# Slot logits for three images as one product of 32 columns, with the masking operation reading them three times

## The chip, the cores and the metric

The kernel runs on one core of one Trainium2 chip, in float32 throughout. The metric is the device time of one execution in microseconds (us). Engines go by short names: PE is the matrix engine (its weight loads are listed as PEld), DVE the vector engine, ACT the scalar engine, POOL the GpSimd engine, SP the engine that issues the DMAs.

## The reference, cut to what matters

A small vision model in three stages: patches are normalised and projected to tokens (32 images, 36 tokens each, 192 channels); attention over channels with a residual and a layer norm; then a soft mixture of experts with 8 experts of 4 slots. The change lies in the last stage:

```python
Xn = l2_normalize(X, axis=-1)                       # X: [32, 36, 192]
sp = l2_normalize(slot_params, axis=1) * scale      # [192, 8, 4]
logits = jnp.einsum('bmd,dnp->bmnp', Xn, sp)        # 32 logits for each token
D = softmax(logits, axis=1)                         # over the tokens of one image
C = softmax(logits.reshape(b, m, 32), axis=2)       # over the 32 slots of one token
X_tilde = einsum('bmd,bmnp->bnpd', Xn, D); ...      # experts on the slots
Y = jnp.einsum('bnpd,bmnp->bmd', Y_tilde, C)
```

The slots `sp` are the same for all images.

## The kernel before, in words

The images are worked in 11 groups of three (`NG = 11`, `GI = 3`; the last group has two). A group is 108 tokens, which lie on 108 partitions. So that one set of operations serves three images, a group's router works on a matrix of 108 tokens by 96 columns, 96 being 3 images times 32 slots, in which only the block of a token's own image counts; everything else gets -1e30 added (`negmask`) before the exponentials.

The slots are prepared once: `slot_sums`, `slot_root` and `slot_scale` normalise them, and a loop of three vector operations (L779 to L782) writes them three times side by side into `sp3`, a tile of 96 partitions and 2 x 3 x 32 elements (the 192 channels are split into two halves of 96, index `f`).

For each group g the router then runs:

- `turn_xn` (L579, PE) turns the unit tokens, and `take_xn` (L1111, ACT) copies them to `xnT`.
- `logits` (L593, PE): for each half f, `xnT` is the weight operand (96 rows by 108 columns) and `sp3[:, f]` the moving operand of 96 columns. A float32 product is two PE instructions in the profile, so a group has 4 of them, and 11 groups 44. They write `ps[0:108, 6, 0:96]`.
- `mask_logits` (L890, DVE) adds `negmask` to the 96 columns and writes `lm`.
- `turn_l` (L606, PE), the maxima `max_c` and `max_d` (L897, L905, DVE), the exponentials (L1118, L1126, ACT), `invert_sums` and `scale_d` (L912, L913, L918, DVE), `turn_dc` (L622, L623, PE), `take_d` (L926, DVE) and `slot_in` (L634, PE).

The experts follow: `hidden` (L649, PE), `gelu`, `spread` (L935, DVE), then `slot_out` (L664, PE), `slot_bias`, `combine` (L677, PE) and a last layer norm.

No planner runs: each engine has a fixed list of calls, written out by hand (PE at L680 to L699, DVE at L983 to L1036), and works it in that order; semaphores tell it when an input is there. The products of the attention stage of later groups are interleaved with the router of earlier ones. The slots are prepared at the `slot_scale()` of L991, long before `logits(0)` at L686.

Of the kernel before, what the change touches and what calls it, by code (L numbers as in the profile page):

```python
# [25 lines left out]
ALU = mybir.AluOpType  # L26
# [10 lines left out]
GI = 3  # L37
NG = (B + GI - 1) // GI
NT = NTOK // 128
F = D // 2  # L40
R = D - 128
NE, NP = 8, 4
SL = NE * NP
# [9 lines left out]
def images(g):  # L53
    return min(GI, B - g * GI)


def tokens(g):
    return images(g) * TOK
# [16 lines left out]
def build(nc, x, x_t, w_tok, ln1_gb, ln2_g, ln2_b, g2col, b2col, w_qk, w_v, w_rest, w_proj, b_proj, temp, slots, scale,  # L75
# [3 lines left out]
    with ctx:  # L79
        def sb(name, shape):  # L80
            return ctx.enter_context(nc.sbuf_tensor(name, shape, F32))

        def sem(name):
            return ctx.enter_context(nc.semaphore(name))
# [4 lines left out]
        negmask = sb("negmask", [128, GI * SL])  # L89
# [16 lines left out]
        spsq = sb("spsq", [F, 2, NE, NP])  # L106
        spn = sb("spn", [F, 2, NP])
        spe = sb("spe", [F, 2, NP])
        sp3 = sb("sp3", [F, 2, GI, NE, NP])
        scl = sb("scl", [F, 1])  # L110
        wd = sb("wd", [F, 2, NE, 32])
        bd = sb("bd", [128, 2])
# [49 lines left out]
        NX = 3  # L162
        xnT = sb("xnT", [F, NX, 2, GI * TOK])
        lm = sb("lm", [128, NX, GI * SL])
# [24 lines left out]
        ps = ctx.enter_context(nc.psum_tensor("ps", [128, 8, 512], F32))  # L189
# [38 lines left out]
            return ps[0:F, 5, 0:2 * GI * TOK].rearrange("p (f n) -> p f n", f=2)[:, :, 0:tokens(g)]  # L228

        def lgp(g):  # L230
            return ps[0:tokens(g), 6, 0:images(g) * SL]

        def ltp(g):
            return ps[0:images(g) * SL, 6 if g < GS else 0, 0:tokens(g)]
# [44 lines left out]
        sp_ready = sem("sp_ready")  # L279
# [52 lines left out]
        lm_ready = sem("lm_ready")  # L332
# [115 lines left out]
        def _(pe):  # L448
# [134 lines left out]
            def logits(g):  # L583
                pe.wait_ge(xnT_ready, g + 1)
                if g == 0:
                    pe.wait_ge(sp_ready, 1)
                    pe.wait_ge(y1_ready, NT)
                if 1 <= g <= GS:
                    pe.wait_ge(eD_ready, g)
                if g > GS:  # L590
                    pe.wait_ge(lm_ready, g)
                for f in range(2):
                    mm = pe.matmul(lgp(g), xnT[:, g % NX, f, 0:tokens(g)],  # L593
                                   sp3[:, f, 0:images(g), :, :].rearrange("p i n q -> p (i n q)"),
                                   start=f == 0, stop=f == 1)
                mm.then_inc(lgp_ready, 1)

# [86 lines left out]
            project(1); qkv(5); mix(2); norms(4); turn_h(7); project(2); qkv(6); mix(3); gram(4)  # L684
            norms(5); turn_h(8); project(3); qkv(7); mix(4); norms(6); gram(5); turn_xn(0); project(4)
            logits(0); qkv(8); mix(5); norms(7); gram(6); turn_l(0); turn_xn(1); project(5); qkv(9)  # L686
            mix(6); gram(7); norms(8); logits(1); turn_dc(0); turn_xn(2); project(6); turn_l(1)
            norms(9); gram(8); qkv(10); gram(9); logits(2); turn_xn(3); mix(7); turn_l(2); slot_in(0)
            turn_xn(4); norms(10); logits(3); project(7); turn_dc(1); turn_l(3); logits(4); turn_xn(5)
            mix(8); slot_in(1); turn_xn(6); turn_l(4); logits(5); turn_dc(2); project(8); turn_l(5)  # L690
# [12 lines left out]
        def _(dve):  # L703
# [64 lines left out]
            def slot_scale():  # L768
                dve.wait_ge(sp_root, 1)
                dve.tensor_scalar(spn[:, :, :], spe[:, :, :], EPS_L2, None, ALU.add).then_inc(sp_eps, 1)  # L770
                dve.wait_ge(sp_eps, 1)
                dve.reciprocal(spe[:, :, :], spn[:, :, :]).then_inc(sp_inv, 1)
                dve.wait_ge(sp_inv, 1)
                for f in range(2):
                    ins = dve.tensor_tensor(spsq[:, f, :, :], spraw[:, f, :, :],
                                            spe[:, f, :].unsqueeze(1).broadcast_to([F, NE, NP]), ALU.mult)
                ins.then_inc(sp_scaled, 1)
                dve.wait_ge(sp_scaled, 1)
                for i in range(GI):  # L779
                    ins = dve.tensor_scalar(sp3[:, :, i, :, :].rearrange("p f n q -> p f (n q)"),  # L780
                                            spsq[:, :, :, :].rearrange("p f n q -> p f (n q)"),
                                            scl[:, 0:1], None, ALU.mult)  # L782
                ins.then_inc(sp_ready, 1)

            def scales(g):
                ni = images(g)
# [93 lines left out]
                                  ALU.mult, ALU.mult).then_inc(xn_ready, 1)  # L880

            def mask_logits(g):
                n, s = tokens(g), images(g) * SL
                dve.wait_ge(lgp_ready, g + 1)
                if g >= NX:
                    dve.wait_ge(eC_ready, g - NX + 1)
                    dve.wait_ge(ltp_ready, g - NX + 1)
                if g == 0:
                    dve.wait_ge(negmask_in, 16)
                dve.tensor_tensor(lm[0:n, g % NX, 0:s], lgp(g), negmask[0:n, 0:s], ALU.add).then_inc(lm_ready, 1)  # L890

            def max_c(g):
                n, s = tokens(g), images(g) * SL
# [95 lines left out]
            token_moments(4); x_stats(6); slot_sums(); x_moments(6); token_out(5); turn_p(0); x_stats(7)  # L989
            token_stats(5); token_out(6); x_moments(7); token_moments(5); x_stats(8); x_moments(8)  # L990
            scales(1); y_sums(0); token_stats(6); scores(1); slot_scale(); score_max(1); ln2_norm(4)  # L991
            y_norm(0); token_moments(6); score_shift(1); token_out(7); ln2_norm(5); turn_p(1)
            token_stats(7); scales(2); ln2_norm(6); scores(2); token_moments(7); residual(0)
# [5 lines left out]
            scores(4); score_max(4); residual(3); score_shift(4); h1(1); h1_length(1); turn_p(4)  # L999
            h1_length(2); scales(5); unit_h1(0); h1_inverse(1); h1(2); y_sums(4); unit_h1(1); y_norm(4)  # L1000
            scores(5); score_max(5); residual(4); mask_logits(0); score_shift(5); residual_stats(3)
            turn_p(5); residual_stats(4); residual_moments(3); scales(6); h1_inverse(2); y_sums(5)
            y_norm(5); unit_h1(2); scores(6); h1(3); residual_moments(4); score_max(6); max_d(0)
            score_shift(6); max_c(0); residual(5); h1_length(3); turn_p(6); residual_stats(5)
            h1_length(4); scales(7); h1(4); invert_sums(0); scale_d(0); h1_inverse(3); y_sums(6)
            residual_moments(5); scores(7); y_norm(6); mask_logits(1); max_c(1); score_max(7)
            unit_h1(3); score_shift(7); scales(8); residual(6); max_d(1); h1_length(5); h1(5)
            residual_stats(6); turn_p(7); scores(8); h1_inverse(4); residual_moments(6); unit_h1(4)
            h1_inverse(5); invert_sums(1); score_max(8); scale_d(1); score_shift(8); take_d(0)
            h1_length(6); unit_h1(5); scales(9); mask_logits(2); h1(6); scores(9); h1_inverse(6)  # L1010
            y_sums(7); max_d(2); unit_h1(6); score_max(9); max_c(2); y_norm(7); score_shift(9)
            turn_p(8); mask_logits(3); invert_sums(2); max_c(3); scale_d(2); residual(7); take_d(1)
# [339 lines left out]
```

## Time and profile before

| | |
|---|---|
| time, median of 3 runs | 112.63 us (112.24 to 112.75) |
| the profiled execution's own time | 112.18 us |
| its span, first to last instruction | 110.4 us |
| PE busy | 101.7 us, 92% |
| DVE busy | 87.7 us, 79% |
| ACT busy | 67.5 us, 61% |
| POOL busy | 53.4 us, 48% |

The span is the stretch that the trace covers; 1.8 us of the profiled execution's time lie around it. A busy PE is one that has an instruction in its pipeline: the instructions overlap, so the mean duration of one is longer than the distance at which one follows another. To read that distance (the pitch), divide a stretch of equal instructions on the chain of waits by their number, or compare two starts in the timeline.

### The profile page before, as it was taken

How to read it: one execution, taken by the hardware profiler on the slowest of the kernel's cores; microseconds unless marked ns; L12 is line 12 of the kernel's file. 1: busy time of each engine (PE TensorE's matmuls, PEld its weight loads, DVE VectorE, ACT ScalarE, POOL GpSimd, SP SyncE). 2: the span in 40 equal slices, each digit the busy share in tenths (PEclk: the TensorE clock that was granted, in tenths of full speed). 3: DMA queues.
4: the chain of work that ended last, by engine and by line, in shares of the span. 5: the costliest groups of instructions: out<-in, count | busy, mean ns of one | idle time of the engine just before them, and what ended most of it. 6: DMA issues, size and time to landing. Idle time of an engine off the chain costs nothing. (4 is left out here: it accounts for less than half of the span.)

```text
span 110.4 us, 4479 instructions
## 1 busy us (share of the span) xinstructions
PE 101.7 (92%) x1607; PEld 88.2 (80%) x1607; DVE 87.7 (79%) x380; ACT 67.5 (61%) x222; POOL 53.4 (48%) x126
## 2 busy tenths in 40 slices
PE   6999999999999999999999999799989989999900
PEld 6999989979999887887898887679779668879500
DVE  2129756968998958958977989999999897999960
ACT  4000023729563887798887996787785994476570
POOL 8800552263999887847204417906030340076880
PEclk9999999999999999999999999999999999999996
DMA  2999999469501111111000000010042000002232
GB/s 23 334 339 394 389 386 398 153 212 342 235 0 30 36 32 40 29 35 32 6 3 6 0 6 0 6 48 24 30 105 72 7 0 3 0 6 84 66 112 58
DMA packets 8554, 11.27 MB, mean 102 GB/s; under 512 B 2358, under 2 KB 5878, under 8 KB 8534
## 3 DMA queue, kind: packets, MB, share of 16 engines
q1 hardware_dynamic: 8533, 11.00, 29.5%
q8 instruction: 13, 0.21, 0.8%
q14 instruction: 8, 0.06, 0.2%
HBM read 9.22 MB, written 0.88 MB: 92 GB/s over the span
## 5 line engine op out<-in xcount | busy, mean ns | idle before, releaser
L480 PE MATMUL ps<-wc,xT 128*128 128x192 f32 x108 | 19.1, 330 | 0.0
L480 PEld LDWEIGHTS ps<-wc,xT 128*128 128x128 f32 x108 | 17.4, 190 | 0.7 <-issue 0.6
L1046 ACT ACTIVATE hT<-ps,b,g 128x128 f32<-128x128 f32 x18 | 7.3, 463 | 16.4 <-PE ps L491 16.3
L1068 ACT ACTIVATE km<-ps,imgsel 108x192 f32<-108x192 f32 (+1 forms) x32 | 11.1, 420 | 3.7 <-PE ps L515 3.6
L1256 POOL TENSOR_SCALAR mv<-mv 108x1 f32<-108x1 f32 (+1 forms) x11 | 3.0, 270 | 14.4 <-DVE mv L856 14.4
L568 PE MATMUL ps<-wp,yT 128*108 128x192 f32 (+1 forms) x44 | 9.3, 333 | 0.0
L664 PE MATMUL ps<-wu,hb 128*96 128x192 f32 (+1 forms) x44 | 9.2, 332 | 0.1
L1261 POOL TENSOR_TENSOR r<-mv,halves 108x2 f32<-108x2 f32 (+1 forms) x11 | 8.8, 803 | 0.8
L508 PE MATMUL ps<-wqk,hT 128*108 128x192 f32 (+1 forms) x44 | 9.0, 326 | 0.0
L726 DVE BATCH_NORM_STATS2 st<-xs 128x6 f32<-128x384 f32 x18 | 8.9, 537 | 0.0
L1249 POOL TENSOR_TENSOR rqt<-rn,tempc 128x6 f32<-128x6 f32 x11 | 2.2, 199 | 12.1 <-ACT rn L1105 12.1
L1207 POOL TENSOR_SCALAR var<-mv 128x1 f32<-128x1 f32 x9 | 2.0, 219 | 11.8 <-DVE mv L731 11.5
L1078 ACT ACTIVATE sqk<-km 108x576 f32<-108x576 f32 (+1 forms) x11 | 7.5, 683 | 0.0
L664 PEld LDWEIGHTS ps<-wu,hb 128*96 128x96 f32 (+1 forms) x44 | 6.5, 161 | 0.8 <-issue 0.4
L593 PE MATMUL ps<-sp,xnT 96*108 96x96 f32 (+1 forms) x44 | 6.2, 264 | 0.7 <-ACT xnT L1111 0.4
L568 PEld LDWEIGHTS ps<-wp,yT 128*108 128x108 f32 (+1 forms) x44 | 6.4, 170 | 0.5 <-DVE yT L836 0.2
L559 PE MATMUL ps<-vT,pc 32*32 32x37 f32 x512 | 6.8, 195 | 0.0
L1162 ACT ACTIVATE o<-z,sh,rstd 108x192 f32<-108x192 f32 x10 | 5.1, 543 | 2.8 <-DVE sh L980 2.8
L1269 POOL TENSOR_TENSOR rstd<-var,mhalf 108x1 f32<-108x1 f32 (+1 forms) x11 | 6.3, 576 | 0.9
L506 PE MATMUL ps<-hT,wv 128*128 128x108 f32 (+1 forms) x44 | 6.6, 273 | 0.0
L559 PEld LDWEIGHTS ps<-vT,pc 32*32 32x32 f32 x512 | 5.5, 104 | 1.3
L508 PEld LDWEIGHTS ps<-wqk,hT 128*108 128x108 f32 (+1 forms) x44 | 6.4, 171 | 0.0
(118 smaller groups left out, 296.6 us busy)
## 6 DMA issues: line engine op xcount, KB each, us to landing
xT<-in_x_t SPq DMA_DIRECT2D x9, 384.0 KB, 6.4
xs<-in_x SPq DMA_DIRECT2D x9, 384.0 KB, 6.2
out<-o SPq DMA_DIRECT2D x10, 81.0 KB
wt<-in_w_tok SPq DMA_DIRECT2D x2, 288.0 KB, 3.2
wqk<-in_w_qk SPq DMA_DIRECT2D x1, 192.0 KB, 5.9
wp<-in_w_proj SPq DMA_DIRECT2D x1, 192.0 KB, 10.0
wd<-in_w_down SPq DMA_DIRECT2D x1, 192.0 KB
z<-h SPq DMA_DIRECT2D x2, 81.0 KB
```

Source lines behind the costliest of these rows:

```text
L480: mm = pe.matmul(tokp(t), xT[:, o + kc * 128:o + (kc + 1) * 128], wc[:, kc, :], start=kc == 0, stop=kc == KC - 1)
L506: pe.matmul(vp(g)[:, m, :], wv[:, m, :], main, start=True, stop=False)
L508: pe.matmul(qkp(g)[:, m, :], main, wqk[:, m * D:(m + 1) * D], start=False, stop=False)
L559: mm = pe.matmul(yp(g)[r, m, i, :], pc[r, g % 2, GI * m + i, :], vT[r, m, g * GI + i, :], start=True, stop=True, tile_position=(32 * j, 32 ...
L568: mm = pe.matmul(prp(g), yT[:, g % NY, m, 0:images(g), :].rearrange("p i n -> p (i n)"), wp[:, m, :], start=m == 0, stop=m == 1)
L664: mm = pe.matmul(ytp(g), hb[:, e, i0:i0 + ni, :, :].rearrange("p i n q -> p (i n q)"), wu[:, e, :], start=e == 0, stop=e == 1)
L726: ins = dve.bn_stats(st1[:, t % 2, h, :], xs[:, t % NB, h * (PD // 2):(h + 1) * (PD // 2)])
L1046: ins = act.activation(hT[:, f, t * 128:(t + 1) * 128], htp(t)[:, f, :], ACT.Identity, bias=b2[:, f:f + 1], scale=g2[:, f:f + 1])
L1068: act.activation(km[0:n, g % NK, i, :], qkp(g)[:, 1, :], ACT.Copy, scale=imgsel[0:n, i:i + 1])
L1078: act.activation(sqk[0:n, g % 2, 0:ni, :], km[0:n, g % NK, 0:ni, :], ACT.Square).then_inc(sqk_ready, 1)
L1261: pool.tensor_tensor(r3[0:n, g, :], mv3[0:n, g, 1:3], halves[0:n, :], ALU.pow).then_inc(r3_ready, 1)
L1269: pool.tensor_tensor(rstd4[0:n, g:g + 1], var4[0:n, g:g + 1], mhalf[0:n, 0:1], ALU.pow).then_inc(rstd4_ready, 1)
```

## The change

The slots are stored once (`spk`, 2 x 32 elements a partition). The moving operand of `logits` has 32 columns instead of 96 (64 in the last group), and the product fills 32 columns of PSUM. The masking operation reads these 32 columns once for each image of the group, by a middle dimension of stride 0, and writes 96 columns as before. Two of the three vector operations that stored the slots are gone. Semaphores, the order of the calls and everything behind `lm` stay as they are.

```diff
-        sp3 = sb("sp3", [F, 2, GI, NE, NP])
+        spk = sb("spk", [F, 2, NE, NP])
...
         def lgp(g):
-            return ps[0:tokens(g), 6, 0:images(g) * SL]
+            return ps[0:tokens(g), 6, 0:SL]
...
                     mm = pe.matmul(lgp(g), xnT[:, g % NX, f, 0:tokens(g)],
-                                   sp3[:, f, 0:images(g), :, :].rearrange("p i n q -> p (i n q)"),
+                                   spk[:, f, :, :].rearrange("p n q -> p (n q)"),
                                    start=f == 0, stop=f == 1)
...
-                for i in range(GI):
-                    ins = dve.tensor_scalar(sp3[:, :, i, :, :].rearrange("p f n q -> p f (n q)"),
-                                            spsq[:, :, :, :].rearrange("p f n q -> p f (n q)"),
-                                            scl[:, 0:1], None, ALU.mult)
-                ins.then_inc(sp_ready, 1)
+                dve.tensor_scalar(spk[:, :, :, :].rearrange("p f n q -> p f (n q)"),
+                                  spsq[:, :, :, :].rearrange("p f n q -> p f (n q)"),
+                                  scl[:, 0:1], None, ALU.mult).then_inc(sp_ready, 1)
...
-                dve.tensor_tensor(lm[0:n, g % NX, 0:s], lgp(g), negmask[0:n, 0:s], ALU.add).then_inc(lm_ready, 1)
+                dve.tensor_tensor(lm[0:n, g % NX, 0:ni * SL].rearrange("p (i s) -> p i s", i=ni),
+                                  lgp(g).unsqueeze(1).broadcast_to([n, ni, SL]),
+                                  negmask[0:n, 0:ni * SL].rearrange("p (i s) -> p i s", i=ni),
+                                  ALU.add).then_inc(lm_ready, 1)
```

## Rows read from the trace of the kernel before

**Rows 1.** Busy time by stretch; columns: stretch, length, engines, granted clock, DMA share, GB/s.
```profile
20.00:68.00 48.00, 48.00 (x990) 41.70 (x991) 40.70 (x163) 37.14 (x122) 28.57 (x64) 1.00 0.20 65
70.00:84.00 14.00, 12.86 (x274) 10.96 (x273) 13.96 (x81) 10.88 (x50) 4.42 (x9) 1.00 0.19 46
88.00:98.00 10.00, 9.50 (x70) 7.95 (x72) 8.78 (x39) 5.71 (x21) 2.36 (x5) 1.00 0.00 1
...
104.00:110.40 6.40, 0.94 (x4) 0.28 (x3) 2.89 (x14) 2.50 (x5) 3.02 (x8) 0.84 0.30 86
```

**Rows 2.** PE's waits from 68 to 88 us: total, times, longest, in us.
```profile
PE ps L606 <- DVE lm L890: 0.6, 1, 0.6
PE ps L622 <- DVE dm L926: 0.3, 1, 0.3
```

**Rows 3.** The chain of waits in order of time: start us, us, what.
```profile
72.95 0.59 PE ps L593 x4
...
76.15 0.19 PE ps L579 x2
...
80.70 0.34 PE ps L634 x4
81.04 0.39 PE ps L593 x4
...
89.01 0.62 PE ps L593 x4
...
92.83 0.25 PE ps L593 x4
```

**Rows 4.** PE's timeline from 28.5 us: start, us, instruction, shapes, count.
```profile
29.00 0.59 PE L506 MATMUL ps<-hT,wv 128*128 128x108 f32 x4
29.43 0.82 PE L508 MATMUL ps<-wqk,hT 128*108 128x192 f32 x4
```

**Rows 5.** PE's instructions by line and shape (weights rows*columns, moving rows x columns).
```profile
L593 PE MATMUL ps<-sp,xnT 96*108 96x96 f32 x40 | 5.8, 268 | 0.7 <-ACT xnT L1111 0.4 <-ACT eD L1126 0.2
L634 PE MATMUL ps<-dm,xn 108*96 108x96 f32 x40 | 5.2, 253 | 0.0
L579 PE MATMUL ps<-ident,xn 108*96 108x108 f32 x20 | 3.6, 260 | 0.0
L649 PE MATMUL ps<-xt,wd 96*32 96x96 f32 x32 | 0.9, 251 | 0.0
L649 PE MATMUL ps<-xt,wd 96*32 96x32 f32 x32 | 0.5, 200 | 0.0
```

**Rows 6.** DVE's timeline about L890 of the eighth group.
```profile
81.27 0.14 DVE L913 RECIPROCAL rD<-sD 96x1 f32<-96x1 f32 x1
81.45 0.26 DVE L890 TENSOR_TENSOR lm<-ps,negmask 108x96 f32<-108x96 f32 x1
```

**Rows 7.** DVE's instructions by line and shape (out<-in, partitions x elements).
```profile
L836 DVE TENSOR_TENSOR yT<-ps,rden 128x216 f32<-128x216 f32 x10 | 3.8, 376 | 0.3
L844 DVE TENSOR_TENSOR z<-ps,z 108x192 f32<-108x192 f32 x10 | 3.5, 349 | 1.4 <-PE ps L568 1.3
L890 DVE TENSOR_TENSOR lm<-ps,negmask 108x96 f32<-108x96 f32 x10 | 2.5, 246 | 0.4 <-PE ps L593 0.3
L775 DVE TENSOR_TENSOR spsq<-spraw,spe 96x32 f32<-96x32 f32 x2 | 0.3, 184 | 0.0
```

**Rows 8.** DVE's timeline from 35 us.
```profile
35.32 0.92 DVE L780 TENSOR_SCALAR sp<-spsq,scl 96x64 f32<-96x64 f32 x3
36.16 0.29 DVE L807 TENSOR_REDUCE mx<-e 128x6 f32<-128x144 f32 x1
```

**Rows 9.** L780 alone: duration ns min/median/max, first and last start us.
```profile
L780 DVE TENSOR_SCALAR sp<-spsq,scl x3: 241/250/589, 35.3 to 36.0; 96x64 f32<-96x64 f32 x3
```

**Rows 10.** L890 alone from 70 to 84 us: stretch, length, DVE busy, clock, DMA.
```profile
70.00:84.00 14.00, 1.44 (x6) 1.00 0.19 46
```

**Rows 11.** Two products of one shape, by line: busy us, mean ns.
```profile
L452 PE MATMUL ps<-still 128*128 128x192 f32 x12 | 4.2, 541 | 1.1 <-DVE still L704 1.1
L480 PE MATMUL ps<-wc,xT 128*128 128x192 f32 x108 | 19.1, 330 | 0.0
```

More of the change, by code:

```diff
@@ L882, in mask_logits @@
             def mask_logits(g):
-                n, s = tokens(g), images(g) * SL
+                n, ni = tokens(g), images(g)
                 dve.wait_ge(lgp_ready, g + 1)
```

## The prediction, made before the changed kernel was run

> **What bounds the kernel now.** I read the busy time by stretch first [rows 1]. From 20 to 68 us PE is busy for 48.00 of 48.00 us, and the list of PE's waits over that stretch is empty: PE sets the pace there, and DVE, at 40.70 us, has 7.3 us to spare. From 70 to 84 us it is the other way round: DVE is busy for 13.96 of 14.00 us and PE for 12.86. PE's waits [rows 2] say the same, since it stands for 0.6 us for the masked logits (L890) and for 0.3 us for a copy, both DVE's. From 88 to 98 us PE leads again (9.50 of 10), and from 104 us on the last layer norm runs down, with PE nearly idle. So a gain on PE counts in full before 68 us and behind 88 us, a gain on DVE counts between 70 and 84 us. The chain of waits [rows 3] agrees: from 72.95 us on it holds seven pieces of L593, of 4 instructions each, 28 in all; the first and last are shown.
>
> **The products, 44 instructions.** The question is what sets the pitch of L593: its 96 moving columns, which become 32, or its 108 weight columns, which stay. Four pitches from the chain and the timeline, with their shapes from [rows 5] and [rows 4]:
>
> - L634, 96 weight columns and 96 moving: 0.34 / 4 = 85 ns [rows 3]
> - L579, 96 weight and 108 moving: 0.19 / 2 = 95 ns [rows 3]
> - L593, 108 weight and 96 moving: 0.39 / 4 = 97 ns [rows 3]
> - L506, 128 weight and 108 moving: (29.43 - 29.00) / 4 = 107 ns [rows 4]
>
> L593 moves exactly as many columns as L634 and takes 12 ns more; L506 moves exactly as many as L579 and takes 12 ns more. In both pairs only the weights are wider. The pitch follows the wider of the two operands: 85 ns at 96, 95 to 97 at 108, 107 at 128. Each product instruction brings a weight load of its own (990 and 991 of them in the first stretch [rows 1]), and I read the pitch as the time until the next load is in, however short the product beside it. With 108 weight columns and 32 moving the wider is still 108, so the pitch stays at 95 to 97 ns and PE's work stays what it is: 0 gained. The last group has 72 weight columns and moves 64, at 0.25 / 4 = 62 ns [rows 3]; by the same reading it keeps that. Behind a group of logits come products or transposes whose wider operand is 96 or more, so nothing is gained at the seam either.
>
> What does fall is the latency of the last instruction of a group. L649 takes 251 ns with 96 moving columns and 200 ns with 32 [rows 5], so the masking operation is released 51 ns earlier. It counts only where something on the way to the end waits for exactly this. In the eighth group DVE had finished L913 at 81.41 us and began L890 at 81.45 [rows 6], in the full stretch: at most 0.05 us. In the others DVE comes late or PE does not need it at once. I take 0.05 us in the sum; the bound is 51 ns in each of the eight masking operations behind 72 us, 0.4 us.
>
> **The masking operation, 11 times.** It keeps its 96 elements out and its mask of 96 elements in; only the PSUM operand is read by a pattern with a middle dimension of stride 0. No row shows that pattern. The nearest is L836, which reads PSUM in short pieces of 36 and its other operand with stride 0: 376 ns for 216 elements. L844, which reads plainly, needs 349 ns for 192, and L890 246 ns for 96 [rows 7], which is 103 ns for 96 elements, or 1.07 ns an element. By that slope 216 elements are 349 + 26 = 375 ns, so L836's pattern costs 1 ns. I take 0. As a lower end I take 0 as well, since as many elements are written; as the upper end, far off, three short operations instead of one: L775, 32 elements, takes 184 ns, and 3 x 184 - 246 = 306 ns more [rows 7]. That end is a rival below.
>
> **The slots stored once.** L780 starts at 35.32 us, three times over 0.92 us [rows 8], and takes 241, 250 and 589 ns [rows 9]. Two go: between 0.33 us (two of the short kind at a pitch of some 0.16 us) and 0.68 us (the third starts at 36.0, the first at 35.3). DVE's next operations, from L807 on, start that much earlier. This lies where PE never waits and DVE has 7.3 us of slack [rows 1]; what hides the gain is PE's own work, and what is late next is PE again. Counted at 0; if PE did wait for DVE there, 0.33 to 0.68 us would be gained. `sp_ready` comes earlier too, but `logits(0)` stands far behind it in PE's list. No DMA moves, no wait is added, and no queue is changed.
>
> **The sum.** 112.18 us of the profiled execution, less 0.05, is 112.13. That execution lies 0.45 us below the median of the runs, 112.63; on the scale of the runs I forecast 112.63 - 0.05, or rounded 112.6 us. The likeliest case's own range is 111.9 (0.4 of latency and 0.3 of the runs' scatter) to 112.9 us (12 ns on each of the six masks of the full stretch is 0.07 us, and the scatter).
>
> **Rival A, faster: the moving columns set the pitch after all.** For it: the trace has no wide product that moves far fewer columns than it loads; L506's 108 over 128 is the most uneven. Against it: the two pairs above. Scaling L634's 85 ns by 32/96 gives 28 ns, some 32 with a few ns of issue, so an instruction of a full group would save 95 - 32 = 63 ns. Before 70 us three groups have 12 instructions: 0.76 us, in the stretch where PE is full. On the chain behind it are 24 of full groups and 4 of the last: 24 x 63 + 4 x 30 = 1.63 us. Together 2.4 us. Of this, 20 instructions (1.26 us) lie from 72.95 to 81.04 us, where DVE has 0.04 us to spare, so little of them comes through: 1.1 to 2.4 us, and by the row it is nearest to (DVE full) 1.3 us: 111.3 us. The Trainium skill, page "TensorE: Matmul & The Clock Gate", section "Back-to-back issue gap", lists a gap of about 60 cycles for 1 to 64 moving columns, whatever is loaded; taken alone that rule would be this rival. The same section says that a stream of loads and products is spaced by both, which is what the trace shows.
>
> **Rival B, slower: the masking operation pays for each image it reads.** If a stride of 0 in PSUM breaks the read in three, an operation costs up to 306 ns more. Six of them lie between 70 and 84 us [rows 10], where DVE is full, so 6 x 0.306 = 1.8 us and 114.4 us in all. It decides from 0.56 / 6 = 94 ns an operation. Against it is L836, at 1 ns.
>
> **Rival C, slower: PE's clock.** The same number of instructions moves a third of the columns. If the granted clock fell while PE still leads, products would take what L452 takes at the start, 541 ns against L480's 330 for one shape [rows 11], which I read as the lower level though the clock is not marked there; each us of PE's work at the lower level, 1.2 GHz instead of 2.4, costs about another. 0.6 us of it would be enough for slower; over 2 us of PE's work, 114.6 us. For it: the clock does fall to a mean of 0.84 behind 104 us, after PE has gone idle [rows 1]. Against it: it reads 1.00 through 70 to 84 us though PE stands there several times. The Trainium skill, same page, section "A second HAM failure mode: psum-queue depth-cycling", says that many small idle times between groups of products can make the clock swing. Here the idle times do not grow, as the pitch stays.
>
> **Chances.** The forecast (nothing to be seen) 0.76, rival A 0.13, rival B 0.07, rival C 0.04. A change of 0.5%, 0.56 us, is about what can be told from none. Of the forecast's 0.76 I give 0.03 to a gain above that, by latencies that add up, and 0.01 to a loss. So faster 0.16, same 0.72, slower 0.12. The range reaches down to rival A's 111.3, to hold 8 in 10, and ends at 113.0.
>
> **What would show it.** Right: in the new trace L593 has 32 columns, its pieces on the chain still take 0.39 us for four, its mean duration falls by about 50 ns, and its weight loads keep their number and length; L890 stays at 246 ns within 10; L780 is there once and PE's list of waits from 20 to 68 us is still empty. Wrong: four L593 in 0.15 us or so (rival A), L890 above 340 ns (rival B), a granted clock below 1.00 before 100 us (rival C). If DVE's 0.33 to 0.68 us shows at the end, then the stretch before 68 us was not PE's alone.

## The result: 0.7% slower, and a clock that falls in 10 of 22 executions

The changed kernel takes 113.27 us (median of 22 executions, 112.11 to 119.20) against 112.00 us (22, 111.24 to 112.77). In 10 of the 22, PE's granted clock fell for a while to its lower level, as it is not seen to do in the kernel before; eight of these took 118.2 to 119.2 us, the other two 115.26 and 113.34. The ratio is 1.007, 95% interval [1.004, 1.010]; here and below it leaves out the executions that took over 1.5% more than the fastest of their kernel, which are nine of these ten. I call an execution one with a fall when its mean clock is below 0.975, a line that I drew after seeing the results: no execution lies between 0.967 and 0.980. (The clock also falls at the end of every execution, when PE runs out of work, so no mean is 1.00.) The kernel before was at 0.982 or above in all 92 executions whose clock I have beside the experiments. One fall was profiled; of the others I have the mean clock and the time, and not the place.

So two things are to be explained: the falls, and 0.79 us without them (112.79 against 112.00; 0.4 to 1.1 us by the interval). For both, two profiles are needed. The first is the one taken with the result (span 117.0 us, with a fall), the second that of the same kernel run again (112.64 us, span 110.8, without). The clock rows of the page, first with the fall, then without (40 slices, tenths of full speed):

```profile
PEclk9999999999999999999999999555555999999995
```

```profile
PEclk9999999999999999999999999999999999999995
```

Busy time by stretch in the execution with the fall (same columns as [rows 1]):

```profile
20.00:68.00 48.00, 48.00 (x991) 41.57 (x989) 39.96 (x161) 36.96 (x122) 28.93 (x65) 1.00 0.21 65
...
70.00:84.00 14.00, 13.18 (x211) 11.46 (x213) 10.55 (x57) 7.91 (x35) 3.15 (x7) 0.61 0.21 50
```

```profile
74.00:90.00 16.00, 16.00 (x182) 14.13 (x181) 10.39 (x58) 7.89 (x35) 2.65 (x6) 0.50 0.18 41
```

Up to 70 us these rows hardly differ. From about 73 to 90 us the clock is at 1.2 instead of 2.4 GHz. Before it fell PE had stood twice, for 0.60 us at 71 us and for 0.22 us at 72.5, as it does in the kernel before. DVE, full in the kernel before [rows 1], now waits for PE. Its chain of waits shows the price per piece:

```profile
73.26 1.41 PE ps L568 x4
...
75.19 0.59 PE ps L593 x4
...
77.07 0.89 PE ps L634 x4
```

Four L593 take 0.59 us where four took 0.39, and four L634 up to 0.89 where they took 0.34 [rows 3]. Comparing the starts of the same instructions in both traces, PE is 0.24 us ahead of the kernel before at 73 us and 6.35 us behind at 84 us: the fall cost 6.6 us.

Without a fall, the same kernel's rows are these: the page's busy times, L593's products and weight loads, the masking operation and the one store left, and PE's longest wait from 68 to 92 us:

```profile
PE 101.7 (92%) x1607; PEld 88.1 (79%) x1607; DVE 87.1 (79%) x378; ACT 67.3 (61%) x222; POOL 53.5 (48%) x126
```

```profile
L593 PE MATMUL ps<-spk,xnT 96*108 96x32 f32 x40 | 5.3, 254 | 0.7 <-ACT xnT L1112 0.4 <-ACT eD L1127 0.2
L593 PEld LDWEIGHTS ps<-spk,xnT 96*108 96x108 f32 x40 | 4.6, 174 | 1.7 <-issue 0.8 <-ACT xnT L1112 0.7
L888 DVE TENSOR_TENSOR lm<-ps,negmask 108x96 f32<-108x96 f32 x10 | 2.5, 246 | 0.2 <-PE ps L593 0.2
L779 DVE TENSOR_SCALAR spk<-spsq,scl 96x64 f32<-96x64 f32 x1 | 0.7, 665 | 0.0
```

```profile
PE ps L606 <- DVE lm L888: 0.6, 1, 0.6
```

PE's timeline shows the pitch, at the place that answers to the third piece of [rows 3]:

```profile
81.08 0.49 PE L593 MATMUL ps<-spk,xnT 96*108 96x32 f32 x4
81.45 0.26 PE L622 MATMUL ps<-ident,eD 96*108 96x96 f32 x1
```

Four instructions in 0.37 us: 93 ns each with 32 columns, where the chain showed 97 with 96 [rows 3]. That mean hides something. The distances from start to start are 40, 96, 95 and 142 ns in this piece, where they were four times 95: the second product follows the first 55 ns sooner, and the next instruction behind the group starts nearly that much later. In a group that starts after a pause the distances are 116, 95, 95 instead of 170, 95, 95. So the group as a whole takes PE nearly as long as before, but its result is there sooner. Here is the masking operation that belongs to this piece:

```profile
81.61 0.26 DVE L888 TENSOR_TENSOR lm<-ps,negmask 108x96 f32<-108x96 f32 x1
```

It starts 0.53 us after the first product. In the kernel before it was 0.58, from this start to L890's at 81.45 [rows 6]:

```profile
80.87 0.54 PE L593 MATMUL ps<-sp,xnT 96*108 96x96 f32 x4
```

There are still 40 weight loads for the full groups, at 174 ns (173 before). The masking operation takes 246 ns as before, PE waits for it as long as before [rows 2], and PE's busy time in all is 101.7 us in both kernels.

The time without a fall is lost elsewhere. DVE's timeline about the last group's unit tokens (`unit_h1(10)`, L877 after and L879 before), first the kernel after, then the kernel before:

```profile
90.81 0.37 DVE L870 TENSOR_SCALAR z<-z,mv,r 72x192 f32<-72x192 f32 x1
91.09 0.15 DVE L865 RECIPROCAL inv<-nrm 72x1 f32<-72x1 f32 x1
91.71 0.32 DVE L877 TENSOR_SCALAR xn<-z,inv 72x192 f32<-72x192 f32 x1 [0.46 <-DVE inv L865]
```

```profile
90.69 0.37 DVE L872 TENSOR_SCALAR z<-z,mv,r 72x192 f32<-72x192 f32 x1
90.98 0.15 DVE L867 RECIPROCAL inv<-nrm 72x1 f32<-72x1 f32 x1
91.24 0.32 DVE L879 TENSOR_SCALAR xn<-z,inv 72x192 f32<-72x192 f32 x1
```

The same instruction starts 0.62 us after the reciprocal instead of 0.26. The answer's label (it waited for the reciprocal) can't be the reason, since that had ended 0.46 us before. The chain of waits of the kernel after runs through this hole:

```profile
91.17 0.08 DVE inv L865
91.26 0.03 issue
91.28 0.02 DVEq L876
91.31 0.40 issue
91.71 0.33 DVE xn L877
92.03 0.04 issue
92.08 0.33 PE ps L579 x2
```

"Issue" is time in which the engine waited for nothing that the profile shows. From 57 to 90 us PE's starts lag those of the kernel before by 0.06 to 0.34 us, a lag that goes up and down; from here to the end it is 0.44 to 0.47 us. There was a step before it: until 56 us the lag is 0.08 to 0.09 us, at 60 us it is 0.25. DVE's timeline shows a smaller hole there, again first the kernel after, then the kernel before:

```profile
55.64 0.29 DVE L877 TENSOR_SCALAR xn<-z,inv 108x192 f32<-108x192 f32 x1
56.09 0.38 DVE L834 TENSOR_TENSOR yT<-ps,rden 128x216 f32<-128x216 f32 x1 [0.16 <-issue]
```

```profile
55.56 0.30 DVE L879 TENSOR_SCALAR xn<-z,inv 108x192 f32<-108x192 f32 x1
55.78 0.38 DVE L836 TENSOR_TENSOR yT<-ps,rden 128x216 f32<-128x216 f32 x1
```

The second operation starts 0.45 us after the first instead of 0.22. PE's product L568 needs its result and starts 0.34 us after the instruction ahead of it instead of 0.22, although PE counts as busy all through and its list of waits is empty.

### The profile page after: what moved, and what is told of

The parts are those of the page before. It is cut to its first block and busy times, and to the rows that moved or that the text cites. A ratio compares the mean times of both kernels' runs of the same rounds, so it can differ in the third digit from the quotient of the medians.

```text
span 117.0 us, 4477 instructions
## 1 busy us (share of the span) xinstructions
PE 108.4 (93%) x1607; PEld 94.0 (80%) x1607; DVE 89.6 (77%) x378; ACT 67.8 (58%) x222; POOL 53.4 (46%) x126
## 5 line engine op out<-in xcount | busy, mean ns | idle before, releaser
L568 PE MATMUL ps<-wp,yT 128*108 128x192 f32 (+1 forms) x44 | 11.5, 393 | 0.0
L568 PEld LDWEIGHTS ps<-wp,yT 128*108 128x108 f32 (+1 forms) x44 | 7.9, 204 | 0.8 <-DVE yT L834 0.4
L593 PEld LDWEIGHTS ps<-spk,xnT 96*108 96x108 f32 (+1 forms) x44 | 6.6, 217 | 1.7 <-ACT xnT L1112 0.7
L634 PE MATMUL ps<-dm,xn 108*96 108x96 f32 (+1 forms) x44 | 7.6, 310 | 0.0
L593 PE MATMUL ps<-spk,xnT 96*108 96x32 f32 (+1 forms) x44 | 6.9, 286 | 0.7 <-ACT xnT L1112 0.5
L559 PE MATMUL ps<-vT,pc 32*32 32x37 f32 x512 | 7.5, 206 | 0.0
L559 PEld LDWEIGHTS ps<-vT,pc 32*32 32x32 f32 x512 | 6.1, 114 | 1.6 <-issue 0.6
L1140 ACT ACTIVATE xt<-ps 96x192 f32<-96x192 f32 (+1 forms) x11 | 3.5, 318 | 6.3 <-PE ps L634 6.3
```

What stands on the lines that cost most here:

```text
L559: mm = pe.matmul(yp(g)[r, m, i, :], pc[r, g % 2, GI * m + i, :], vT[r, m, g * GI + i, :], start=True, stop=True, tile_position=(32 * j, 32 ...
L568: mm = pe.matmul(prp(g), yT[:, g % NY, m, 0:images(g), :].rearrange("p i n -> p (i n)"), wp[:, m, :], start=m == 0, stop=m == 1)
L593: mm = pe.matmul(lgp(g), xnT[:, g % NX, f, 0:tokens(g)], spk[:, f, :, :].rearrange("p n q -> p (n q)"), start=f == 0, stop=f == 1)
L634: mm = pe.matmul(xtlp(g)[:, f, :], xn[0:tokens(g), g, f * F:(f + 1) * F], dm[0:tokens(g), g % NX, 0:images(g) * SL], start=True, stop=True)
```

## The experiments

Twelve kernels ran, each beside the kernel before. The first four take the change apart. Of each the ratio with its interval and the number of executions with a fall are given. The edits are cut to what matters. The kernels ran in three sets of four, each set on a chip of its own.

**The changed kernel again.**

```diff
(no edit)
```

> The changed kernel again, to get more executions with the granted clock of each. Theory C (the clock: fewer moving columns let PE's granted clock fall to its lower level in some executions): about 4 in 10 executions at a mean clock near 0.91 and near 118.5 us, the rest at 112 to 113.5 us; a stretch at 0.50 begins near 73 us where it happens. Rival B (the masking operation is dearer): L888 above 340 ns in executions with the clock at 1.00 too. Rival S (the slots stored once shift DVE's work): the clock has nothing to do with the 0.7% of the undisturbed executions, and PE's waits between 68 and 95 us differ from those of before.

Ratio 1.0076 [1.0047, 1.0105], 2 of 12 with a fall (118.51 and 114.89 us). The loss repeats; the falls are there but rarer.

**96 columns moved, the rest as changed.**

```diff
-  mm = pe.matmul(lgp(g), xnT[...], spk[:, f] as (n q), ...)
+  k = images(g)
+  mm = pe.matmul(ps[0:tokens(g), 6, 0:k * SL] as (i s), xnT[...],
+                 spk[:, f] as (n q), unsqueeze(1), broadcast_to([F, k, SL]), ...)
```

> The changed kernel, but with the moving operand of the logits read three times (stride 0), so that the product moves 96 columns again; the masking operation still reads 32 columns three times, the slots are still stored once. Theory C: no execution with a lower clock (mean 0.99), and about 112.0 us, the time before. Rival B: 112.8 us as the changed kernel's undisturbed executions, since the masking operation is the same. Rival S: 112.8 us too.

Ratio 1.0046 [1.0013, 1.0078], no fall in 12. By itself that says little, since the changed kernel beside it fell in 2 of 12 only; all kernels together are counted further down. But the ratio stays above 1: theory C alone doesn't explain the rest.

**The slots stored once, and nothing else.**

```diff
+  (product of 96 columns as above)
-  lgp(g).unsqueeze(1).broadcast_to([n, ni, SL]),
+  ps[0:n, 6, 0:ni * SL].rearrange("p (i s) -> p i s", i=ni),
```

> Only the storing is changed: slots stored once, product of 96 columns by a moving operand of stride 0, masking operation plain over 96 columns. Theory C: 112.0 us, clock 0.99. Rival B: 112.0 us. Rival S: 112.8 us.

Ratio 1.003 [1.0002, 1.0057], no fall in 12. This was the surprise: with product and masking as before, the trace has the same hole.

```profile
90.31 0.15 DVE L866 RECIPROCAL inv<-nrm 72x1 f32<-72x1 f32 x1
90.92 0.32 DVE L878 TENSOR_SCALAR xn<-z,inv 72x192 f32<-72x192 f32 x1 [0.46 <-DVE inv L866]
```

So the hole comes with removing two vector operations 55 us earlier. That speaks for rival S, and against B.

**96 columns in the first three groups only.**

```diff
-  k = images(g)                    # as in the kernel with 96 columns above
+  k = images(g) if g < 3 else 1
```

> The changed kernel with 96 moving columns in the first three groups of logits only (those before 70 us) and 32 in the other eight. Theory C, if the moving columns ahead of the pause at 70 us decide: no execution with a lower clock, about 112.0 to 112.3 us. If those behind the pause decide: 3 to 4 in 10 executions at 0.91 and 118 us as before. Rivals B and S: 112.8 us as in the changed kernel.

Ratio 1.0063 [1.0031, 1.0096], 1 of 11 with a fall, a short one (mean clock 0.966, 113.61 us), and none of the long ones.

**A theory for the hole.** In each trace of a kernel with 378 vector instructions I counted DVE's records, semaphore waits included. The hole lies always between the 447th and the 448th. The smaller one (0.22 us for DVE, 0.17 us in PE's starts) lies between the 191st and the 192nd, 256 earlier. In the changed kernel run again, an instruction queue moves eight pieces of 8192 bytes; four of them start at 28.8, 56.7, 76.1 and 92.4 us, each within 1.5 us after DVE passes record 64, 192, 320 or 448. They start behind the holes, so no hole is a wait for one of these; and at record 320 there is no hole. I took it that DVE's instructions come in pieces, that the border between two can cost 0.35 us (the hole with nothing in hand, 0.62 us between two starts instead of 0.26), and that with two instructions fewer the border moved from behind a running 0.37 us operation (L872), which hid it, to a place where DVE had nothing in hand. The Trainium skill, page "Runtime: NRT & Kernel Launch", section "Instruction fetch mechanics", says that each engine's sequencer fetches its instructions by its own DMA in blocks of 256, and that crossing a border is mostly hidden. The distance of 256 between the two holes agrees; the transfers of 8192 bytes, half of the 16 KiB that the section names, don't; and the "mostly" is what failed here.

**DVE's count restored.** The slots are stored three times again, into tiles of which one is used.

```diff
-  dve.tensor_scalar(spk, spsq, scl[:, 0:1], None, ALU.mult).then_inc(sp_ready, 1)
+  for o in (spx, spy, spk):
+      ins = dve.tensor_scalar(o, spsq, scl[:, 0:1], None, ALU.mult)
+  ins.then_inc(sp_ready, 1)
```

> The changed kernel with DVE's instruction count restored: the slots are stored three times again, into three tiles of which one is used; product of 32 columns and masking by stride 0 stay. Theory F (fetch: DVE's stream of instructions is brought in pieces, and two instructions fewer move a border of them onto the critical unit_h1 of the last group, where DVE stood idle for 0.46 us in all four changed kernels profiled at full clock and not in the kernel before): that idle time is gone, and executions without a fall of the clock are 0.4 us shorter than the changed kernel's. Rival M (the masking operation or the product costs it): unchanged at 112.8 us. Theory C (fewer moving columns let the clock fall): falls of the clock in 3 to 4 of 10 executions, as in the changed kernel.

Ratio 1.0009 [0.9972, 1.0046], 2 of 12 with a fall (120.60 us, and 112.74 at 0.967). The hole is gone:

```profile
91.46 0.15 DVE L869 RECIPROCAL inv<-nrm 72x1 f32<-72x1 f32 x1
91.72 0.32 DVE L881 TENSOR_SCALAR xn<-z,inv 72x192 f32<-72x192 f32 x1
```

**The control: the two operations added late.**

```diff
-  last_shift(9); last_out(10)
+  last_shift(9); spare(); last_out(10)     # two tensor_scalar into spx, spy
```

> A control: the changed kernel with the two removed vector operations added at the end of DVE's list, ahead of last_out(10), instead of at the start. Theory F: the count ahead of unit_h1(10) is that of the changed kernel, so its 0.46 us of idle time stays, 112.8 us. Rival (the number of DVE's instructions in all, not their place, decides): the idle time is gone, 112.4 us. Theory C: falls of the clock in 3 to 4 of 10 executions.

Ratio 1.012 [1.0056, 1.0183] from 4 executions, 2 more of 6 with a fall. The hole stays:

```profile
91.37 0.15 DVE L873 RECIPROCAL inv<-nrm 72x1 f32<-72x1 f32 x1
91.98 0.32 DVE L885 TENSOR_SCALAR xn<-z,inv 72x192 f32<-72x192 f32 x1 [0.46 <-DVE inv L873]
```

This kernel has as many vector instructions as the one before it, and the same work; only the number ahead of unit_h1(10) differs. So it is the count ahead that decides, not the count in all, nor the product, nor the masking. (The two operations ahead also take 0.25 us of DVE's time, but DVE is in step again by 40 us.) That the border is one of fetching instructions is the reading that fits the distance; no run shows the fetch itself, nor what hides it where it isn't seen. With the full count the 192nd record follows the 191st by 0.02 us, without a long operation in hand.

Three traces tell what each part costs. The numbers are the lag of PE's starts behind the same instructions of the kernel before, in us (minus: ahead):

| | at 50 us | at 60 us | at 90 us | at 94 us |
|---|---|---|---|---|
| 96 columns, short count (stored once only) | -0.82 | -0.66 | -0.67 | -0.32 |
| 32 columns, short count (changed kernel again) | 0.08 | 0.25 | 0.12 | 0.47 |
| 32 columns, full count (count restored) | 0.62 | 0.62 | 0.48 | 0.48 |

The smaller hole costs 0.17 us and the larger 0.35, with either product, and both are gone with the full count. The 32 columns give 0.13 to 0.14 us back between 60 and 90 us, and the 96 don't.

**Count restored, 96 columns moved.**

```diff
+  (both edits: three stores, product of 96 columns by stride 0)
```

> Count restored as in the first, and the product moves 96 columns by stride 0; only the masking operation differs from the kernel before in what it reads. Theories C and F together: no fall of the clock, no idle time before unit_h1(10), ratio to the kernel before 1.000 within 0.3%. Rival B (masking): 1.003 or more.

Ratio 1.0021 [0.9984, 1.0059]. The masking operation that reads PSUM by stride 0 costs nothing to be seen: its 246 ns [rows 7] in the changed kernel say so more sharply than this ratio, whose interval reaches to 0.6%. Two executions stand out: 128.06 us at a mean clock of 0.757, a fall where theory C wants none, and one of 325.21 us with L482, the token product, at 889 ns instead of 330. The latter is the one that was profiled, and its trace holds no record of the clock at all, so the 1.00 listed for it says nothing; its token products mostly follow one another at 630 ns, where all other traces have 320 at the start and then 162. I have no explanation for either, and so no usable trace of this kernel.

**Count restored, PE kept busy at the pauses.**

```diff
-  for f in range(2):
+  for f in list(range(2)) * {3: 4, 4: 3}.get(g, 1):
       mm = pe.transpose(xntp(g)[:, f, :], xn[...], ident[...])
```

> Count restored, product of 32 columns; turn_xn(3) is issued four times instead of once and turn_xn(4) three times, which gives PE 10 more transposes of 108 columns (0.95 us) just ahead of the two pauses between 70 and 73 us. Theory C (too little moved about the pauses lets the clock fall): no execution with a fall of the clock, and 111.8 to 112.1 us. Rival (it is the logits' own shape and not what PE moves in all): falls in 3 to 4 of 10 executions.

Ratio 1.0005 [0.9965, 1.0044], no fall in 12, with 32 columns. This is the version that loses nothing to be seen; it gains nothing to be seen either.

**The same transposes, in two places.** Two kernels, both with the changed kernel's count, in one comparison.

```diff
+  c1: {3: 4, 4: 3}      (at the pauses)
+  c2: {0: 4, 1: 3}      (ahead of them)
```

> The changed kernel as it is (32 columns, DVE's count short by two) with turn_xn(3) issued four times and turn_xn(4) three times, 10 transposes more (0.95 us) just ahead of PE's pauses between 70 and 73 us. Theory C with its place (what PE does about the pauses decides whether the clock falls): 0 of 12 executions with a fall, where the changed kernel and its control had 14 of 40. Theory F: the idle time before unit_h1(10) stays, so 0.4 us above the kernel before. Rival (the fall comes from the missing DVE instructions): 4 of 12.

> The same 10 transposes, but for turn_xn(0) and turn_xn(1), 7 to 13 us ahead of the pauses, where PE never waits, so they cost 0.95 us. Theory C with its place: the falls stay, 3 to 5 of 12 executions. Rival (what PE moves in the whole kernel decides, wherever it is): 0 of 12. Time of the undisturbed ones: 113.3 to 113.8 us in both.

At the pauses: 1.0066 [1.0035, 1.0096], no fall in 12. Ahead of them: 1.0147 [1.0090, 1.0203], 2 of 6 with a fall (119.92 and 122.10 us). PE's and the other engines' busy time from 70 to 74 us, first at the pauses, then ahead of them:

```profile
70.00:74.00 4.00, 3.96 (x101) 3.40 (x101) 4.00 (x20) 3.19 (x15) 1.84 (x3) 1.00 0.14 37
```

```profile
70.00:74.00 4.00, 3.17 (x91) 2.57 (x91) 4.00 (x21) 3.16 (x16) 1.83 (x3) 1.00 0.12 32
```

Ten transposes fill the pauses in the one, and the fall is not seen; in the other the pauses and the falls stay. My price for the first was too high (113.3 to 113.8 us, measured 112.82): in a pause they cost nearly nothing. The second is a weak control. Six executions are few, and its trace has a further loss that none of the others has: at 75 us DVE stood for 1.03 us for a DMA (`z<-h`), and PE for 0.87 us behind it. PE's lag grows by 0.9 us from 50 to 65 us, of which the smaller hole has 0.17, and by another 1.0 us at 75 us. So the ratio isn't simply the price of ten transposes, and this kernel can have a third pause of PE beside the two.

**64 columns.**

```diff
-  k = images(g)
+  k = 2
```

> The changed kernel with products of 64 columns (stride 0, two images' worth). Theory C: fewer falls than at 32 columns, 0 to 2 of 12; if the fall depends on the logits having 32 columns in another way, 4 of 12. Pitch of L593 95 ns as with 32 and 96 columns.

Ratio 1.0054 [1.0020, 1.0089], no fall in 12.

**96 columns in the two groups at the pauses only.**

```diff
-  k = images(g)
+  k = 3 if 2 <= g <= 3 else 1
```

> The changed kernel with 96 moving columns in the third and fourth groups of logits only (69.5 and 73 us, the two at the pauses), 32 in the other nine. Theory C with its place: 0 or 1 of 12 executions with a fall that starts near 73 us. Rival (all groups count alike): 2 to 4 of 12.

Ratio 1.0031 [0.9995, 1.0067], no fall in 12. Two groups of eleven look to be enough; at the rate of 18 in 58 counted below, 12 executions without a fall come by chance once in some 90 times, at the 8 in 36 of the experiments alone once in 20.

**The falls together.** The kernels that move 32 columns in every group and leave the pauses as they are (the changed one twice, count restored, count late, transposes ahead) fell in 18 of 58 executions. Those with wider products or with transposes at the pauses (a2, a3, b3, b4, c1, c3, c4) fell in 1 of 84 (325.21 us not counted as one), and the kernel before in 0 of 92. Set by set the same comparison is 2 of 12 against 0 of 24, 4 of 18 against 1 of 24, and 2 of 6 against 0 of 36, so it isn't one chip's doing. Left out of both is a4, with wide products in the first three groups only: 1 of 11. It is these sums that show that the falls go with what PE moves; no single kernel's count does. That the place, about the pauses, decides rests on less: on c1 and b4 (0 of 24) against c2 (2 of 6), and on c4.

## Why the prediction was wrong

**Where the time lies.** The forecast was 112.6 us and its range 111.3 to 113.0; measured were 113.27. The falls put it outside: the 12 executions without one have a median of 112.75. But that this lies inside the range is luck, since the base was 0.63 us too high (112.63 by three executions, 112.00 by 22). On the true base the range would have ended at 112.4, and the loss without falls would have missed it too. So two steps failed, and a third had the wrong working.

**What held.** PE's pace is set by the weights: 93 ns a product with 32 moving columns. The masking operation is unchanged at 246 ns. PE's list of waits from 20 to 68 us is empty (but see the smaller hole: the list doesn't show all). The operations behind the stores began 0.25 us earlier, in place of the 0.33 to 0.68 I had set (the one store left took 665 ns), and PE hid it, as forecast: DVE was in step again by 40 us.

**What failed, first: "Counted at 0" for the slots stored once.** The step weighed the two operations by their duration and asked only what hides the gain. It did not ask what their absence moves. By the control and its pair it moved a border in DVE's instruction stream onto unit_h1(10), and that cost 0.35 us on the chain, with 0.17 us at the smaller hole. The kernels with the short count measured 1.003 to 1.012 (the one with transposes ahead of the pauses aside), those with the full count 1.0005 to 1.0021. Of the changed kernel's 0.79 us the two holes explain 0.52, less the 0.13 that the narrow products give back: 0.39 us, or 0.35%. The rest, 0.40 us with an interval from 0.1 to 0.7, stays open. In the one trace without a fall PE was already 0.09 us late at 34 us, where the two kernels are still the same; how late it was there in the other executions is not on record.

**Second: rival C was priced and given 0.04.** It happened in 10 of 22 executions. I had priced it at 114.6 us, for 2 us of PE's work at the lower level; a long fall took 118.2 to 119.2 us, because it lasted from 73 to 90 us and cost 6.6 us. My reason against it was that the kernel before keeps 1.00 through the pauses, and that the idle time does not grow. Both are true of the traces (3.18 us of PE busy from 69 to 73 us after, 3.19 before), and the clock fell all the same. So the step that failed is the last one, "Here the idle times do not grow, as the pitch stays": equal busy and idle times did not keep the clock up. What the runs showed in its place is that the falls go with the columns moved, 32 for 96 in as much busy time: 18 of 58 executions against 1 of 84. A kernel that holds its clock in 92 executions of 92 gives no row that tells how near it is to losing it.

**Third, small: the latency, right in its effect and wrong in its working.** I had the last product of a group 51 ns shorter. It isn't: a product that follows another without a wait takes 259 ns with 32 columns where it took 258 with 96 (the medians of L593), and the mean fell by 14 ns (254 for 268), not by 50. L649's 251 against 200 ns, from which I took it, was of another shape of weights. What shrank is the distance from the first product to the second, by 55 ns, and it releases the masking operation of the eighth group 53 ns earlier, nearly the 51 that I had set. That the number fits is luck. All groups together it was worth 0.13 to 0.14 us, where I had 0.05 in the sum and 0.4 as the bound. "Nothing is gained at the seam" held the other way round: there most of the gain of the first distance is given back.

Rival A is refuted by the pitch (0.37 us for four, not 0.15), though one distance in four did shrink with the moving columns. Rival B is refuted by L888's 246 ns.

## What to carry to other kernels

Narrowing a product below its own weight load bought next to no time on PE here (its result came 0.05 us sooner), and it came with falls of the clock: look for pauses of PE near it, and at the clock of many executions, not of one profile. Removing instructions from an engine shifts everything behind them in its stream, so before a loss or gain of some 0.3 us is put down to the work removed, run the same change with the count kept. The pair of kernels, dummy operations early and dummy operations late, tells the two apart in one run. An engine that counts as busy all through can still be running late: compare the starts of the same instructions in two traces, and look where their difference steps.

## What the runs showed of the hardware that I had not expected

- DVE stood still for 0.46 to 0.48 us at the same record of its stream in all ten profiles with the short count (the one with the count added late among them), and in none of the three with the full count that ran at a usual pace.
- With 32 moving columns instead of 96 under weights of 108 columns, the second product of a group starts 55 ns sooner after the first (40 instead of 95 ns, or 116 instead of 170 after a pause); the later ones keep 95 ns.
- PE's clock, once it fell near 73 us, stayed at its lower level until about 90 us, though PE was busy for 16.00 of 16.00 us from 74 to 90.
- Ten transposes (0.95 us of PE's work) put into the pauses cost 0.02 to 0.13 us: from 60 to 90 us PE's lag changes by -0.11 us with them and -0.13 without (c1 and a1), and by -0.01 with them and -0.14 without (b4 and b1).
- The profiled executions differ early, where the kernels are still the same: the products at the start change from a pitch of 320 to 162 ns at some time between 4.1 and 7.3 us, which leaves a lead or lag of -0.98 to +0.63 us against the kernel before at 8 us. In some it stays to the end (-0.82 of -0.80 at 20 us in a3, 0.62 of 0.63 in b1), in others PE waits for DVE near 15 us and most of it is gone (0.03 of -0.88 in c1). The scatter of 111.2 to 112.8 us of the kernel before may well come of this, but it has one trace only. The clock row doesn't mark the change of pitch.
